# A grouped matrix multiply on one core: the parity of an expert's set counts the number of ranks, and the last stage reads its matrix at fixed addresses

## The reference, cut to what matters

```python
y   = einsum('bsi,boi->bso', x, weight[ids])        # 128 samples, 64 tokens, 1024 -> 1024, 16 experts
h   = einsum('bsd,nrd->nbsr', y, lora_A)            # 8 adapters of rank 16
out = x + einsum('bsd,od->bso', y, W) + bias \
        + einsum('nbsr,nor->bso', h, lora_B * 2 * lora_weights)
```

## Time and profile before

| | us |
|---|---|
| median of 3 runs | 1568.3 |
| the profiled execution | 1567.71 |
| its span, first to last instruction | 1566.0 |
| TensorE matmul busy | 1499.9 (96%) |
| TensorE weight load busy | 1198.7 (77%) |
| VectorE busy | 780.1 (50%) |
| GpSimd busy | 470.0 (30%) |
| ScalarE busy | 387.2 (25%) |
| mean granted TensorE clock | 0.982 of full speed |

### The profile page before, as it was taken

How to read it: one execution, slowest core, us unless ns; L and a number is a source line. 1 busy time by engine, 2 the same in 40 slices (tenths; PEclk the granted TensorE clock), 3 DMA queues, 4 the chain that set the end, 5 groups by cost and what they waited for, 6 DMA issues and landing times.

```text
span 1566.0 us, 28094 instructions
## 1 busy us (share of the span) xinstructions
PE 1499.9 (96%) x6356; PEld 1198.7 (77%) x6357; DVE 780.1 (50%) x1202; ACT 387.2 (25%) x493; POOL 470.0 (30%) x656
## 2 busy tenths in 40 slices
PE   5849999999999999999996999999999999999998
PEld 3738888888888888888874888888888888888886
DVE  6556566766667666377764433333333333333331
ACT  4233333433433333244433110101010101010100
POOL 3433542334433433623332222222222222222221
PEclk9979999999999999999997999999999999999999
DMA  8987678858788776688867655555555555555553
GB/s 230 234 192 162 177 181 186 199 144 198 180 195 198 191 174 158 175 189 191 192 150 202 164 139 147 134 147 134 147 134 147 134 147 134 147 134 147 134 134 80
DMA packets 174549, 257.74 MB, mean 165 GB/s; under 512 B 22720, under 2 KB 130240, under 8 KB 174528
## 3 DMA queue, kind: packets, MB, share of 16 engines
q1 hardware_dynamic: 102944, 138.97, 38.4%
q10 hardware_dynamic: 52000, 76.57, 19.6%
q0 software_dynamic: 19584, 41.98, 9.7%
HBM read 181.93 MB, written 79.69 MB: 167 GB/s over the span
## 4 chain that ended last, share of the span: by engine, by line
PE 82%; DMA 6%; DVE 4%; issue 4%; ACT 2%; ACTq 1%; DVEq 1%; SPq 1%; POOLq 0%; POOL 0%
PE ps L632 27%; PE ps L633 27%; PE ps L634 27%; DMA w_raw<-in_L_cond_weight_dram 3%; DVE w_turn L437 1%; DVE w_lo L507 1%; DMA x_raw<-in_x_dram 1%; DVE x_turn L527 1%; ACT w_hi L333 1%; DMA w_raw<-weff 1%; DMA coef<-_L_ffn_lora_weights_dram 1%; SPq L192 1%; DMA weff<-stage 0%; ACT x_hi L341 0%; POOL x_raw L179 0%
## 5 line engine op out<-in xcount | busy, mean ns | idle before, releaser
L632 PE MATMUL ps<-w_hi,x_hi 128*128 x2096 | 832.8, 397 | 32.0 <-ACT stage L358 21.7
L633 PE MATMUL ps<-w_lo,x_hi 128*128 x2096 | 831.8, 397 | 0.0
L634 PE MATMUL ps<-w_hi,x_lo 128*128 x2096 | 831.5, 397 | 0.0
L632 PEld LDWEIGHTS ps<-w_hi,x_hi 128*128 128x128 f32 x2096 | 395.7, 189 | 130.0 <-issue 34.4
L634 PEld LDWEIGHTS ps<-w_hi,x_lo 128*128 128x128 f32 x2096 | 395.6, 189 | 96.1
L633 PEld LDWEIGHTS ps<-w_lo,x_hi 128*128 128x128 f32 x2096 | 395.8, 189 | 95.6
L179 POOL DMA_DIRECT2D x_raw<-in_x_dram x576 | 308.5, 540 | 508.1 <-DVE x_turn L527 364.2
L341 ACT ACTIVATE x_hi<-x_turn 128x512 fp32r<-128x512 f32 x272 | 160.2, 626 | 762.7 <-DVE x_turn L527 439.2
L313 POOL TENSOR_TENSOR stage<-stage,w_raw 128x1024 f32<-128x1024 f32 x64 | 154.0, 2407 | 566.1 <-DMA stage<-in_x_dram 566.1
L527 DVE STREAM_TRANSPOSE x_turn<-x_raw 128x256 f32<-128x256 f32 x544 | 193.7, 415 | 162.4 <-DMA x_raw<-in_x_dram 113.4
L534 DVE TENSOR_TENSOR x_lo<-x_turn,x_hi 128x512 fp32r<-128x512 f32 x272 | 177.4, 689 | 167.0 <-ACT x_hi L341 165.7
(11 more groups left out here) (75 smaller groups left out, 26.5 us busy)
## 6 DMA issues: line engine op xcount, KB each, us to landing
w_raw<-in_L_cond_weight_dram SPq DMA_DIRECT2D x256, 256.0 KB, 5.8
x_raw<-in_x_dram POOLq DMA_DIRECT2D x576, 64.0 KB, 3.0
y_scr<-stage ACTq DMA_DIRECT2D x144, 256.0 KB, 3.9
x_raw<-y_scr SPq DMA_DIRECT2D x128, 256.0 KB, 2.7
stage<-in_x_dram SPq DMA_DIRECT2D x128, 256.0 KB, 3.7
out_dram<-stage ACTq DMA_DIRECT2D x128, 256.0 KB, 2.9
weff<-stage ACTq DMA_DIRECT2D x8, 512.0 KB, 6.9
weff<-in_L_ffn_W_dram POOLq DMA_DIRECT2D x8, 512.0 KB, 14.9
```

The costliest lines, as they stand in the source:

```text
L632: mm(ps[b][:, cols], x_hi[b][:, t, :], hi, start=t == 0, stop=False)
L633: mm(ps[b][:, cols], x_hi[b][:, t, :], lo, start=False, stop=False)
L634: last = mm(ps[b][:, cols], x_lo[b][:, t, :], hi, start=False, stop=t == KT - 1)
```

## The change

The matrix of rank k now lies in set (k + n_ranks) % 2, so that weff, of rank n_ranks, always lies in set 0. Each engine that needs the set of an expert reads n_ranks from its table and computes the parity with it (`place`). Stage two passes the constant 0, and `products` then builds its moving operands at fixed addresses. The set of rank 0 is no longer known when the program is written, so ScalarE waits for the tables before it rounds the first matrix, and the scratch moves from w_lo's set 1 into the ring of x_hi and x_lo behind its first buffer, which now lies in one arena with hi and lo of a buffer side by side.

```diff
+        def place(eng, rank):
+            return (rank + entry(eng, n_ranks, 0, EXPERTS)) % 2
@@ memory
-        spare = base + 3 * EXPERT_BYTES
+        ring = -(-nc.sbuf_base // 64) * 64
+        ring_arena = sb("ring_arena", [P, (2 * RING * TILE_BYTES + ring - nc.sbuf_base) // 4], f32)
+        x_hi = [... offset=ring + 2 * b * TILE_BYTES ...]
+        x_lo = [... offset=ring + (2 * b + 1) * TILE_BYTES ...]
+        spare = ring + 2 * TILE_BYTES
@@ ScalarE
                     rank = entry(act, slot_rank, 2 * slot, EXPERTS - 1)
+                    par = act.snap(place(act, rank + 1))
                     act.wait_ge(tile_done, slot + FOLDS)
-                    round_w(rank + 1, (rank + 1) % 2)
+                    round_w(rank + 1, par)
...
             move_fold(0)
+            act.wait_ge(tables, 1)
+            first = act.snap(place(act, 0))
             for c in range(CHUNKS // 2):
-                round_w(0, 0, [c])
+                round_w(0, first, [c])
...
             act.wait_ge(tile_done, FOLDS)
-            act.wait_ge(tables, 1)
-            round_w(1, 1)
+            round_w(1, act.snap(place(act, 1)))
@@ VectorE
             nc.vector.memset(counts[:, 0, 0:1], 0.0).then_inc(tables, 1)
+            dve.wait_ge(tables, 1)
+            first = dve.snap(place(dve, 0))
...
-                    prepare_w(rank + 1, (rank + 1) % 2)
+                    prepare_w(rank + 1, dve.snap(place(dve, rank + 1)))
...
-            prepare_w(0, 0, ...)       # twice
-            prepare_w(1, 1)
+            prepare_w(0, first, ...)   # twice
+            prepare_w(1, dve.snap(place(dve, 1)))
@@ TensorE
                     for t in range(KT):
-                        hi = w_hi[:, bass.ds(par, 1), t, cols].rearrange("p a m -> p (a m)")
-                        lo = w_lo[:, bass.ds(par, 1), t, cols].rearrange("p a m -> p (a m)")
+                        if isinstance(par, int):
+                            hi, lo = w_hi[:, par, t, cols], w_lo[:, par, t, cols]
+                        else:
+                            (as before)
...
-                        products(u, rank % 2, rank * CHUNKS)
+                        products(u, pe.snap(place(pe, rank)), rank * CHUNKS)
...
-            par = pe.snap(ranks % 2)
...
-                products(u, par, ready)     # both places of stage two
+                products(u, 0, ready)
```

More of the change, by code:

```diff
@@ L67, in grouped_adaln_ffn_kernel @@
         w_lo = nc.alloc_sbuf_tensor_at("w_lo", [P, 2, KT, D], f32r, offset=base + 2 * EXPERT_BYTES)
-        spare = base + 3 * EXPERT_BYTES
+        TILE_BYTES = KT * P * 4
+        ring = -(-nc.sbuf_base // 64) * 64
+        ring_arena = sb("ring_arena", [P, (2 * RING * TILE_BYTES + ring - nc.sbuf_base) // 4], f32)
+        x_hi = [nc.alloc_sbuf_tensor_at(f"x_hi{b}", [P, KT, P], f32r, offset=ring + 2 * b * TILE_BYTES) for b in range(RING)]
+        x_lo = [nc.alloc_sbuf_tensor_at(f"x_lo{b}", [P, KT, P], f32r, offset=ring + (2 * b + 1) * TILE_BYTES) for b in range(RING)]
+        spare = ring + 2 * TILE_BYTES
         a_sb = nc.alloc_sbuf_tensor_at("a_sb", [P, D], f32, offset=spare)
@@ L77, in grouped_adaln_ffn_kernel @@
         x_turn = [sb(f"x_turn{h}", [P, KT // 2, P], f32) for h in range(2)]
-        x_hi = [sb(f"x_hi{b}", [P, KT, P], f32r) for b in range(RING)]
-        x_lo = [sb(f"x_lo{b}", [P, KT, P], f32r) for b in range(RING)]
         stage = [sb(f"stage{b}", [P, D], f32) for b in range(2)]
@@ L91, in scratch @@
             spare_at[0] += -(-n // 64) * 64
-            assert spare_at[0] <= spare + EXPERT_BYTES
+            assert spare_at[0] <= ring + 2 * RING * TILE_BYTES
             return nc.alloc_sbuf_tensor_at(name, shape, dt, offset=at)
@@ L539, in prepare_next_expert @@
                     rank = entry(dve, slot_rank, 2 * slot, EXPERTS - 1)
-                    prepare_w(rank + 1, (rank + 1) % 2)
+                    prepare_w(rank + 1, dve.snap(place(dve, rank + 1)))
                 with dve.Else():
                     dve.nop()
-            prepare_w(0, 0, range(0, CHUNKS // 2))
+            prepare_w(0, first, range(0, CHUNKS // 2))
             prepare_x(0, 0, 0, 0)
-            prepare_w(0, 0, range(CHUNKS // 2, CHUNKS))
+            prepare_w(0, first, range(CHUNKS // 2, CHUNKS))
             for n in range(1, AHEAD):
                 prepare_x(n, n, n % 2, n // 2)
-            prepare_w(1, 1)
+            prepare_w(1, dve.snap(place(dve, 1)))
             with dve.Fori(0, SLOTS // RING - 1) as g:
@@ L629, in products @@
                     for t in range(KT):
-                        hi = w_hi[:, bass.ds(par, 1), t, cols].rearrange("p a m -> p (a m)")
-                        lo = w_lo[:, bass.ds(par, 1), t, cols].rearrange("p a m -> p (a m)")
+                        if isinstance(par, int):
+                            hi, lo = w_hi[:, par, t, cols], w_lo[:, par, t, cols]
+                        else:
+                            hi = w_hi[:, bass.ds(par, 1), t, cols].rearrange("p a m -> p (a m)")
+                            lo = w_lo[:, bass.ds(par, 1), t, cols].rearrange("p a m -> p (a m)")
                         mm(ps[b][:, cols], x_hi[b][:, t, :], hi, start=t == 0, stop=False)
@@ L665, in _ @@
                     pe.wait_ge(out_added, t - (RING - 1))
-                    products(u, par, ready)
+                    products(u, 0, ready)
 _INS = ['x', 'itok_B_0_15', 'L0_cond_weight', 'L0_ffn_lora_A', 'L0_ffn_lora_B', 'L0_ffn_W', 'L0_ffn_bias',
```

## The result

The changed kernel is slower: 1573.9 us against 1568.8, median of six runs each, ratio 1.0034 (95% interval 1.0021 to 1.0047). The forecast was 1552, faster; the time lies inside the range of 1543 to 1577 but on the other side of no change, and is that of rival B, which had 0.38.

What follows compares the result with a forecast made beforehand. TensorE was taken to bound both stages. From 1567.7 us, 20.9 saved in stage two, 3.2 added at VectorE's openings and 1.5 at the start gave 1551.5, with 0.6 to the median some 1552; range 1543 to 1577.

Steps and rivals of the forecast that it cites:

- rival B: Stage two: the address doesn't matter to the array and the added loads remain; 1573 us, chance 0.38.
- What bounds the kernel: Both stages: TensorE is busy nearly throughout, so only a matmul that streams faster can shorten stage two.
- the lead of its sequencer: TensorE's sequencer runs about 4 us ahead of the array, so removing its register work can't shorten stage two.
- 20.9 us of stage two at fixed addresses: Stage two: fixed addresses save 6.8 ns on each of 3063 matmuls, 20.9 us.
- the filler: Fixed-address matmuls of unused slots: 388 ns against stage two's 395, taken as the 7 ns a fixed address saves.
- what is left is the address, or x against w: Filler's 7 ns: accumulation ruled out as cause, leaving address form or operand buffer; forecast took the saving for fixed addresses.
- My argument against B: Both stages: VectorE's and ScalarE's load changed but the 395 ns never did, so placement and traffic seem not to matter.
- The statement on memory: New buffer places: hold nothing longer than the old, and the matrices lie where they lay; 0 us.
- The added loads: Register reads of n_ranks, about 0.8 us each: 3.2 us on VectorE's openings plus 1.5 at the start.
- start of the fourth tile: Start, before 100.78 us: added reads on ScalarE, VectorE and TensorE delay it 1.5 us, between 0.4 and 2.8.
- four openings on the chain: VectorE's last four expert openings, leading into the pause between stages: 4 x 0.8 = 3.2 us longer.
- TensorE's sequencer in stage one: Each used slot: the added read stays under the 4 us lead and costs nothing, 3 us in all as far bound.

Runs made afterwards that it cites:

- e2: Kernel before with only stage two's matmuls put at fixed addresses: 1569.6 us, ratio 1.0001.
- e6: Changed kernel with stage two's moving operand taken from x_hi at a fixed address instead of w: 1555.3 us.
- e15: Kernel before with x_hi and x_lo allocated ahead of the arena of w, nothing else changed: 1528.5 us, ratio 0.9742.
- e1: Changed kernel with the constant 16 in place of reading n_ranks: 1570.2 us, ratio 1.0007.
- e8: Kernel before in which only TensorE reads n_ranks, in each used slot: 1570.4 us, ratio 1.0013.
- e17: Kernel before with an unused 96-byte tile ahead of x_hi, so x_hi and x_lo begin at multiples of 128: 1565.9 us, ratio 0.9979.
- e3: Changed kernel with all its register loads, but stage two addresses its matrix by a register again: 1575.4 us, ratio 1.0037.
- e7: Kernel before in which only VectorE reads n_ranks, at each opening in the slots' loop: 1570.3 us, ratio 1.0006.
- e18: e17 with fewer register loads: slot_opens holds the rank itself, and TensorE reads slot_rank ahead of its waits: 1561.5 us.
- e5: Changed kernel with 48 filler matmuls instead of 2 in each unused slot: no total time given, fillers 226.7 ns apart.
- e11: Changed kernel with stage two's stationary operand taken from w too, so both operands lie in w: 1552.9 us.
- e16: Changed kernel with the start of the arena of x rounded up to 128 instead of 64 bytes: 1571.6 us, ratio 1.0014.
- e14: Changed kernel with stage two's half tiles pairing chosen areas of w, and x_hi with x_lo: no total time given, tiles 10.88 to 10.91 us apart.
- e10: Changed kernel with the arena of x in front of that of w, same computation: 1555.6 us, ratio 0.9929.

## Why the prediction was wrong

**What bounds the kernel: right.** TensorE bounds both stages, the lead of its sequencer exists, and removed register arithmetic saved nothing (e2).

**The term that failed is the 20.9 us of stage two at fixed addresses. It measured 0.** Its size rested on the filler, and the step that failed is the sentence "what is left is the address, or x against w", together with the choice of the first. The filler differed from the stream in two things that I named, and the rows told them apart no better than that; nothing in them spoke for the address. My argument against B, that traffic changed through the stages and the 395 ns never did, excludes traffic. It doesn't exclude place, which is the same all through. e6 shows the 7 ns with w's place exchanged for x's and the address form kept, e15 shows them with the register form kept.

**The statement on memory, "nothing", was right for this change** (233.3 ns before and after), by luck: x moved from byte 184480 to 147648, and had the arenas changed places, it would have been the largest term.

**The added loads: 4.7 us forecast; the whole loss, from loads, layout and the wait for the tables together, is 5.1 us by the medians, and 5.9 by the spans of the two profiles.** By place, in the profiles:

| | forecast | measured |
|---|---|---|
| start of the fourth tile | +1.5 (0.4 to 2.8) | +2.3 |
| four openings on the chain | +3.2 | +2.1 over the first three steps, and 0.6 ahead of the first; 1.1 given back behind the last |
| TensorE's sequencer in stage one | 0, at most 3 | gaps of 0.5 and 1.5, where x came late |
| clock | not named | 0.7 in stage two, 0.4 in stage one |

The chain left TensorE at 662.57 and came back at 840.65 before, 178.1 us:

```profile
662.57 1.03 ACT stage L358
```

After, at 666.09 and 845.71, 179.6:

```profile
666.09 1.03 ACT stage L366
...
672.88 1.26 DVE w_turn L446
...
784.84 1.26 DVE w_turn L446
...
793.88 7.72 DMA w_raw<-weff
...
845.71 0.79 PE ps L646
```

From 672.88 to 784.84 are 111.96 us, against 109.89 in the earlier trace rows. The 62.0 us from 778.65 to 840.65 became 60.9: behind the last opening the chain waits for transfers (of weff 7.72 us), which do not begin later by all that VectorE is later. So 1.5 us of the forecast's 3.2 arrived, and not all of them need be the loads': the three steps take 109.8 to 111.4 us in the five profiles without VectorE's added reads (before, e1, e2, e8, e17) and 111.6 to 112.0 in the three with them (the change, e3, e7), 1.3 more in the mean. The rest of the 5.9 is 2.3 at the start, the gap of about 0.6 at 530 us, some 0.6 by which the path from 103.05 to 666.09 is longer otherwise, of which two more matmuls at half clock are 0.4, and 0.7 in stage two, where twelve matmuls behind the pause ran at half clock instead of nine; 0.1 is left over. The gap at 811 cost nothing, since the pause follows.

The start is the least certain of these. The profiles with the change's beginning have the fourth tile at 102.4 to 105.8 us; those of e2, e8, e15, e17 and e18, with the old one, at 100.2 to 101.0, but e7, with the old one too, at 103.1. e1, without any load, has 102.4, so that part of the start's loss is the wait for the tables or the layout; it was not taken apart.

**B as I wrote it** had the right time, 1573, and one right reason, that the loads remain. Its explanation of the filler, "both its operands lie in x", holds for the filler (e5, e6) and stood there at 0.38 beside a wrong forecast. It is not all of it: both in w is as fast (e11), and in e15 x with w is.

**Open.** Why x stationary with w moving is slow in one layout and not in another. What was seen (start bytes within a partition as allocated, stationary with moving, ns a matmul): x 184480 with w 16512, 233.3; x 147648 with w 16512 to 147583, 233.3; x 184576 with w 16512 (e17), 232.4; x 147712 with w 16512 (e16), 232.4 and then 233.3; x 16512 with w 49344, 228.9; x 16512 with w 49280, 226.7; w with x 147648, 228.9; w with w and x with x, 226.7. Remainders alone don't order these (e16, e17), nor does distance (e14), and since the cadence changed within the profile of e16, the same addresses can have more than one cadence. The times of e17 and e10, which scatter by 9 and 15 us, would fit that, but only one execution of each was profiled. The starts in the trace's whole nanoseconds show a little more: the gaps at 226.7 are even (226, 227, 227), 228.9 is a pattern of three (226, 229, 232 in e10), and 232.4 one of seven (241, 232, 231, 232, 228, 230, 233 in e17). What sets the pattern no run here shows, and I have no mechanism for it.

## What to carry to other kernels

When a stream of equal instructions is the bound, compare its cadence with every other instruction of the same kind and shape in the trace, and list all in which they differ before one is named; here a few ns in 233 were worth 41 us, and a run that exchanges one operand settles it. Where tiles lie in on-chip memory is such a difference: move an allocation and look at the cadence, in more than one execution, before rewriting code around it. A value that an engine reads again in every turn belongs in a register ahead of the loop if the engine is on a chain that sets an end; and a sequencer's lead is only there where nothing upstream is late.

## What the hardware showed beyond that

- A split-format matmul of 512 columns with its weight load came each 226.7, 228.9, 232.4 or 233.3 ns at full clock, by the places of its operands, though not by them alone: in e16 it went from 232.4 to 233.3 within a stage. At half clock it was 427 ns at each of the four (e15, e10, e17, before).
- A matmul whose moving operand's address comes from a register takes as long as one at a fixed address (395 and 395 to 396 ns, e2).
- A register load of one number with its checks took 0.62 us of VectorE's sequencer, from load to load on the chain. The load alone is mostly 0.30 us, with outliers: the 64 reads of n_ranks on TensorE's sequencer in stage one of the changed kernel took 302, 310 and 847 ns (shortest, median, longest).
